# Last expert stage: the gated product kept in a PSUM bank and its high half cast by ScalarE; value rows loaded one block later

## The reference

```python
def _swiglu(u, w1, w2, w3):
    h = jnp.einsum('...d,hd->...h', u, w1)
    v = jnp.einsum('...d,hd->...h', u, w2)
    return jnp.einsum('...h,dh->...d', jax.nn.sigmoid(h) * h * v, w3)
...
_, top_idx = jax.lax.top_k(gate, K)          # K = 4 of E = 8 experts, H = 682
...
out = _swiglu(x, Ws1, Ws2, Ws3)
h1 = jnp.einsum('bsd,ehd->ebsh', x, W1)
h2 = jnp.einsum('bsd,ehd->ebsh', x, W2)
eo = jnp.einsum('ebsh,edh->ebsd', jax.nn.sigmoid(h1) * h1 * h2, W3)
out = out + jnp.einsum('ebsd,bse->bsd', eo, weights)
```

## Time and profile before

| what | us |
|---|---|
| median of 3 runs | 2198.45 (2197.81 to 2206.12) |
| the profiled execution, its own time | 2205.24 |
| its span | 2203.4 |
| PE busy | 1618.1 (73%) |
| DVE busy | 1422.0 (65%) |
| POOL busy | 798.5 (36%) |
| ACT busy | 704.8 (32%) |
| packs of the last stage, first matmul to last | about 575 |

### The profile page before, as it was taken

The page is one execution under the profiler, slowest core; times in us unless marked ns, Lnnn a source line. Parts: engine busy times, 40 slices in busy tenths (PEclk is TensorE's granted clock), DMA queues, the critical chain, the costliest instruction groups (busy, mean ns, idle before and its releaser), DMA issues. The chain is left out here.

```text
span 2203.4 us, 38903 instructions
## 1 busy us (share of the span) xinstructions
PE 1618.1 (73%) x13182; PEld 1262.8 (57%) x13182; DVE 1422.0 (65%) x2628; ACT 704.8 (32%) x1457; POOL 798.5 (36%) x956
## 2 busy tenths in 40 slices
PE   5956766499975768622948996599588888888881
PEld 3545644377752445411634563488588888888881
DVE  4844555666646655541247885566498888888886
ACT  2311011245531434410312664111244444444440
POOL 1421103620014300103314301188566666666660
PEclk8978788689987887855968997699799999999995
DMA  3464615443116332291225321221355445544525
GB/s 103 161 176 124 184 46 148 157 122 114 48 58 184 73 69 68 61 307 61 63 67 170 104 81 37 68 92 66 140 179 177 155 164 177 173 152 171 181 100 191
DMA packets 286765, 274.02 MB, mean 124 GB/s; under 512 B 59033, under 2 KB 263676, under 8 KB 280958
## 3 DMA queue, kind: packets, MB, share of 16 engines
q1 hardware_dynamic: 274647, 249.09, 36.5%
q0 software_dynamic: 8688, 21.16, 2.7%
q10 hardware_dynamic: 3264, 1.57, 0.4%
HBM read 194.74 MB, written 79.35 MB: 124 GB/s over the span
## 5 line engine op out<-in xcount | busy, mean ns | idle before, releaser
L89 PE MATMUL psum<-e_x_split,e_up_split 128*128 128x256 f32 x2340 | 342.5, 300 | 103.7 <-POOL e_up_split L1788 103.7
L89 PEld LDWEIGHTS psum<-e_x_split,e_up_split 128*128 128x128 f32 x2340 | 319.7, 206 | 110.8 <-issue 87.9
L787 DVE TENSOR_REDUCE a_maxima<-psum 128x2 f32<-128x512 f32 x384 | 257.4, 687 | 160.1 <-PE psum L578 91.9
L1788 POOL TENSOR_TENSOR e_up_split<-e_up_raw,e_up_split 128x512 fp32r<-128x512 f32 x195 | 261.0, 1339 | 214.7 <-ACT e_up_split L1710 213.7
L758 ACT ACTIVATE a_probs<-psum 128x512 f32<-128x512 f32 x384 | 224.8, 598 | 265.6 <-PE psum L600 171.2
L1680 PE MATMUL psum<-e_down_split,e_hidden_split 128*128 128x256 f32 x1170 | 183.5, 295 | 0.8 <-DVE e_down_split L1745 0.8
L1731 ACT ACTIVATE e_silu<-psum 128x256 f32<-128x256 f32 x195 | 75.1, 385 | 325.2 <-PE psum L89 325.2
L1680 PEld LDWEIGHTS psum<-e_down_split,e_hidden_split 128*128 128x128 f32 x1170 | 163.1, 201 | 1.0 <-DVE e_hidden_split L1767 1.0
L578 PE MATMUL psum<-s_k_stack,s_q_stack 96*128 96x256 bf16 x512 | 123.0, 295 | 42.2 <-DMA a_rel_stack<-scr_r 30.0
L1767 DVE TENSOR_TENSOR e_hidden_split<-e_hidden,e_hidden_split 128x256 fp32r<-128x256 f32 x195 | 138.8, 712 | 6.7
L1039 DVE TENSOR_TENSOR a_products<-psum,mask 128x512 f32<-128x512 f32 x128 | 82.9, 686 | 77.6 <-PE psum L972 77.4
(11 more groups left out here) (246 smaller groups left out, 3170.6 us busy)
## 6 DMA issues: line engine op xcount, KB each, us to landing
e_up_raw<-in_w_ffn SPq DMA_DIRECT2D x39, 1280.0 KB, 7.5
e_down_raw<-in_w_ffn SPq DMA_DIRECT2D x39, 640.0 KB, 4.1
scr_q<-p_parts SPq DMA_DIRECT2D x40, 384.0 KB, 2.7
scr_k<-p_parts SPq DMA_DIRECT2D x40, 384.0 KB, 2.8
a_q_stack<-scr_q SPq DMA_DIRECT2D x96, 128.0 KB, 2.9
s_q_stack<-scr_q SPq DMA_DIRECT2D x96, 128.0 KB, 2.7
s_k_stack<-scr_k SPq DMA_DIRECT2D x96, 128.0 KB, 2.7
a_k_stack<-scr_k SPq DMA_DIRECT2D x84, 128.0 KB, 3.0
```

Source lines behind the costliest of these rows:

```text
L89: last = eng.matmul(out, lhs(a, k), rhs(b, k), start=i == 0, stop=i == len(terms) - 1)
L787: dve.tensor_reduce(MX[:, u // 8, :, u % 8], s_bank(u), AX.X, ALU.max).then_inc(S["s_used"], 1)
L1788: pool.tensor_tensor(SU[:, r, 1, q], RU[:, r, q], SU[:, r, 0, q], ALU.subtract).then_inc(S["up_lo"], 1)
```

## The change

In the last expert stage the gated product no longer goes to the SBUF tile `hidden` (two buffers) but to the first 256 columns of PSUM bank 3 (one buffer), which no other instruction of the stage uses. Its high half is made by an ACT instruction in place of DVE's copy. It stands on ACT's list between `high_down` and `high_up`, and waits for the product of the same step and for `use_hidden` of two steps before. On DVE's list the order becomes product, `low_down`, at m = 2 `low_x`, then the subtraction for the low half, and at m = 2 `take_out`. As there is one buffer, each product waits for the subtraction of the step before.

In the rows stage the 16 loads of image 0's value rows are issued after block 2 instead of after block 1, and wait for three spills of v instead of two.

```diff
-                        if scr_v is not None:
-                            sp.wait_ge(v_spilled, 32)
-                            stacks.load_v(sp, scr_v, 0)
+                    if stacks is not None and scr_v is not None and n == 2:
+                        sp.wait_ge(v_spilled, 48)
+                        stacks.load_v(sp, scr_v, 0)
...
-        GF = ph.sbuf("hidden", [P, 2, PACK4])
+        hidden = ps[:, 3, 0:PACK4]
...
                         high_down(i, m)
+                        act.wait_ge(S["hidden"], c + 1)
+                        if c >= 2:
+                            act.wait_ge(S["used"], c - 1)
+                        act.activation(GS[:, 0, c % 2], hidden, ACT.Copy).then_inc(S["g_hi"], 1)
                         if i + 1 < packs:
                             high_up(i + 1, m)
...
                         dve.wait_ge(S["silu"], c + 1)
-                        if c >= 2:
-                            dve.wait_ge(S["g_lo"], c - 1)
-                        dve.tensor_tensor(GF[:, c % 2], ps[:, c % 2, PACK4:2 * PACK4], SL[:, c % 2], ALU.mult).then_inc(S["hidden"], 1)
-                        if c >= 2:
-                            dve.wait_ge(S["used"], c - 1)
-                        dve.wait_ge(S["hidden"], c + 1)
-                        dve.tensor_copy(GS[:, 0, c % 2], GF[:, c % 2]).then_inc(S["g_hi"], 1)
+                        if c:
+                            dve.wait_ge(S["g_lo"], c)
+                        dve.tensor_tensor(hidden, ps[:, c % 2, PACK4:2 * PACK4], SL[:, c % 2], ALU.mult).then_inc(S["hidden"], 1)
+                        low_down(i, m)
+                        if m == 2 and i + 1 < packs:
+                            low_x(i + 1)
                         dve.wait_ge(S["g_hi"], c + 1)
-                        dve.tensor_tensor(GS[:, 1, c % 2], GF[:, c % 2], GS[:, 0, c % 2], ALU.subtract).then_inc(S["g_lo"], 1)
-                        low_down(i, m)
+                        dve.tensor_tensor(GS[:, 1, c % 2], hidden, GS[:, 0, c % 2], ALU.subtract).then_inc(S["g_lo"], 1)
                         if m == LAG and i:
                             take_out(i - 1)
-                        if m == 2 and i + 1 < packs:
-                            low_x(i + 1)
```

## The result

The changed kernel takes 2282.74 us (median of 4 runs, 2277.99 to 2283.88), the kernel before 2198.13 on the same chip (2196.65 to 2206.12). The ratio is 1.0373 [1.0344, 1.0402]: 3.7% slower. The direction was predicted, the size was not: 85 us instead of 38, and the time lies above the range. The profiled execution of after took 2277.99, its span is 2276.2.

What follows compares the result with a forecast made beforehand. PE was taken to wait at 38 pack boundaries for POOL's last up-weight tile, late because of ACT. Idle 25 plus clock 14 minus rows 1 gave 38 us, so 2236 us, range 2200 to 2265.

Steps and rivals of the forecast that it cites:

- The mechanism: Pack boundary: the cast makes ACT's high_up(3) 0.66 us later, and POOL's low_up and scatter pass that to PE.
- DVE's relief: Expert stage: DVE loses 195 copies and waiting in the subtraction, over 100 us busy time, with no gain in the sum.
- The idle term: Pack boundaries: PE starts 0.66 us later at each of 38, 25 us in all, bounds 22 to 36.
- The cast's other wait: ACT, step 3: the wait for use_hidden of two steps before ends earlier than the product, about 0.83 against 0.92 us.
- The clock term: Packs: longer PE idle time lets fewer packs escape the 1.2 GHz level; 14 us taken, between 0 and 19.
- 13 cheap ones: Of the 38 pack spacings before, the 13 of 14.02 us or less; all turning dear was put at 19 us.
- dear pack: One of 25 packs with spacing between 15.1 and 15.41 us, partly at 1.2 GHz, costing 1.3 to 1.55 us.
- The third rival: Packs: longer idle time brings a second low-clock stretch in each, 57 us beyond the 38, 2293 us; chance 8%.
- DVE's backlog: Rival at the pack boundary: late DVE holds PE, so relief wins up to 38 us, 2160 us; chance 7%.
- The scatter: Rival at the pack boundary: POOL's scatter hides the later high_up, leaving only the rows stage's effect, 2197 us; chance 12%.
- The rows stage: Projection: loads start at 682 to 685, end at 690 to 693, SP becomes the bottleneck; 1 us won, 0 to 3.
- The subtraction: DVE, expert stage: with one SBUF source it takes about 0.43 us and is no longer held up.

Runs made afterwards that it cites:

- late2: Kernel before with two extra ACT copies at step 3 ahead of high_up, nothing else of the change: 2283.72 us, ratio 1.0361.
- cast_last: Changed kernel with the new cast moved behind high_up on ACT's list: 2186.38 us, ratio 0.9916.
- fill_after: Changed kernel with 20 extra PE matmuls, results unused, ahead of each pack's first: 2184.66 us, ratio 0.9918.
- fill_old: Kernel before with 16 extra PE matmuls, results unused, ahead of each pack's first: 2168.2 us, ratio 0.9861.
- up_ahead_old: Kernel before, rows stage as changed, with the next pack's high_up and low_up taken ahead; product in SBUF, copy on DVE: 2247.71 us, ratio 1.0213.
- up_ahead: Changed kernel with the next pack's high_up and low_up taken ahead on ACT and POOL, cast last in the step: 2064.6 us, ratio 0.9358.
- dve_ahead: The changed kernel's taking-ahead order (up_ahead) with the cast on DVE, read from PSUM: 2176.95 us, ratio 0.9883.
- dve_cast: Changed kernel with the cast given back to DVE, read from PSUM ahead of the subtraction: 2228.38 us, ratio 1.0116.
- late1: Kernel before with one extra ACT copy at step 3 ahead of high_up: 2239.66 us, ratio 1.0164.

## Why the prediction was wrong

- **The mechanism held.** ACT's list makes high_up(3) late, POOL hands that on, PE waits. High_up(3) moved by 0.64 (predicted 0.66), PE's idle time before L89 is 125.0 (predicted 125 to 130), and DVE's relief of 200 us brought no gain. late2 shows that the delay alone is enough, cast_last that without it nothing is lost.
- **The idle term, 25 us, was nearly right.** It measured 21 (38 x 0.55), and the bounds 22 to 36 missed it by 1. The 0.1 us a pack that is missing is the scatter, shorter or earlier than before. It goes with DVE's relief, of which the prediction says "in the sum it is worth nothing". In cast_last, where nothing covers it, the idle time shows it (2.38 against 2.47), and the kernel is 19 us faster than before.
- **The cast's other wait**, for use_hidden of two steps before, "ends earlier" as predicted at step 3. At steps 0 and 1 it did not: it is 43.0 of the 68.8 us that ACT waits before the cast. These steps are not on the path to PE's start.
- **The clock term was the mis-sized one.** I had 14 us, between 0 and 19. The 38 spacings grew by 77 us, idle time explains 21, so the clock took 56; by the ratios of the filled kernels it is up to 70. fill_after and fill_old show that it was the clock: filled, the kernels are 12.5 to 21 us apart instead of 85.
- **The step that failed** is "If all 13 cheap ones turn dear, that costs 13 x 1.45 = 19 us", which gave the term an upper end. It took a dear pack as the worst there is. Behind it stands a wrong reading of the earlier trace rows: "in the dear case twelve matmuls take 2.90 us instead of 1.67". The dear spacing given for it, 1652.39 to 1667.78, is that of a pack whose twelve take 1.68, and the 2.90 belong to the next pack. So the low clock came at two places of a pack, each worth 1.3 to 1.55 us, and nothing in the rows kept a pack from having both. After, nearly every pack has both, at 2.64 us. The third rival had the rest of it, 38 x 1.5 = 57 more, at 8%; 2293 was its time and 2282.74 came. I held against it that "no spacing of before is above 15.41". That was a reading at 2.5 us of idle time, and said nothing on 3.0. In the trace its second stretch joins the first, so that one of 6.0 us of work stands where there was one of 3.1. Why both come at 3.0 us of idle time stays open.
- **The other rivals.** DVE's backlog did not bound: its relief gave no gain. The scatter hid nothing of step 3's delay but gave back 0.1. "DVE stands in neither row" is wrong by the letter: the earlier trace rows has its L1780, behind the packs, at 1%, and L1752 at 0%.
- **The rows stage.** Loads from 683.17 (predicted 682 to 685), through at 690.9 (690 to 693), SP the bottleneck: right. 1.5 us were won in that trace, and the whole cannot be told from nothing.
- **The subtraction** with one source in SBUF was never held: its 195 take 404 to 426 ns in after, where the maximum was 1468. The rule weighed in the prediction (the Trainium skill, "SBUF — State Buffer", section "Who interferes with whom") agrees with the trace, and PE did not wait for it. The prediction put that rule short: the page frees an instruction with at most one SBUF input only outside the modes that use both ports, and DVE's copy, with one, was held in up_ahead_old.

The Trainium skill, "TensorE: Matmul & The Clock Gate", section "HAM oscillation — how this bites in real kernels", tells of a kernel in which each short run of matmuls is followed by a wait, so that PE falls back and pays the low clock at every tile. The trace agrees in kind: from the fifth spacing on the drop is paid in every pack, 2.64 us for 3.02 us of idle time. In before and cast_last it comes in part of the packs already at waits of 2.38 to 2.50 us, shorter than those that the section shows.

## What to carry to other kernels

When PE waits at the same place in every round, the price of a longer wait is not the wait. Here 0.55 us more of idle time cost 2.0 us a pack. Find every place of a round at which the granted clock is low in some of the rounds, price each, and let the clock term reach up to all of them in each round; read so, before gives 1.54 and 1.29 us in 38 packs, or 108 us, of which 35 were paid already; the 73 that are left stand against 56 to 70 measured. A dummy run of matmuls in the gap tells the two apart in one experiment, and can win time by itself. Before moving work to an engine with slack, look at what stands behind it on that engine's list: the same cast ahead of high_up cost 85 us and behind it cost nothing. And relief of an engine that hardly anybody waits for is worth little until the order is changed. Then the packs' part of the change was what carried up_ahead (2064.6) over up_ahead_old (2247.7), in two steps: the product in PSUM with DVE's new order gave 2177 (dve_ahead), the cast on ACT the rest.

## What the runs showed of the hardware

- Idle time per pack and granted clock (0.50 is 1.2 GHz). Mean clock from 1610 to 2130: 0.95 at 2.38 us of idle time, 0.92 at 2.47, 0.90 at 2.87 (dve_cast), 0.86 at 2.69 (late1), 0.81 at 3.02, and 1.00 at 0.66 with the gap filled. It is not a smooth function of the idle time: late1 waits less than dve_cast and has the lower clock. What else decides was not settled. In before the low level came at one of two places, from just ahead of a pack's first matmul or from about 1.5 us behind it, and in eight such stretches PE worked at it for 3.1 to 3.4 us; in after the two stand end to end.
- Matmuls whose results nobody uses made the kernel faster: 98 us of 2283.
- A DVE copy in SBUF was held over four POOL instructions (5.94 instead of 0.29 us), and low_down for 2.78. The Trainium skill, "SBUF — State Buffer", section "Who interferes with whom", has the second to issue blocked until the first is through; here, as POOL's instructions follow each other closely, the copy was held by several of them.
- With its source in PSUM the same cast kept to 0.41 us on DVE beside the same run of POOL instructions, and a DVE product written to PSUM took 0.43, against 0.415 into SBUF.
